# One LSTM with a picked cell: the input rows added by TensorE, and h split into three bf16 columns by GpSimd

## The reference

```python
g0 = x[:, 0] @ W_ih[0].T + b_ih[0] + b_hh[0]
h, c = _lstm_activate(g0, c0)
def step(carry, x_t):
    h, c = carry
    sel_in = jnp.concatenate([h, c, x_t], axis=-1)
    logits = sel_in @ W_sel.T + b_sel
    onehot = jax.nn.one_hot(jnp.argmax(logits, axis=-1), Sx, dtype=x_t.dtype)
    g_all = jnp.einsum('bi,sgi->bsg', x_t, W_ih) + jnp.einsum('bh,sgh->bsg', h, W_hh) + b_ih + b_hh
    g = jnp.einsum('bsg,bs->bg', g_all, onehot)
    h2, c2 = _lstm_activate(g, c)
```

## Time and profile before

| | |
|---|---|
| median of 3 runs | 6211.06 us |
| the profiled execution: its time, its span | 6218.48 us, 6216.4 us |
| granted TensorE clock, mean over the span | 0.944 |
| busy share PE, PEld, DVE, ACT, POOL | 87%, 52%, 49%, 17%, 10% |
| products of the cells (L1456) | 59,904, busy 1231.3 us |
| idle products (L1427) | 4,992, busy 1296.7 us |

### The profile page before, as it was taken

The page is one execution under the profiler, slowest core; times in us unless marked ns, Lnnn a source line. Parts: engine busy times, 40 slices in busy tenths (PEclk is TensorE's granted clock), DMA queues, the critical chain, the costliest instruction groups (busy, mean ns, idle before and its releaser), DMA issues. The chain is left out here.

```text
span 6216.4 us, 213415 instructions
## 1 busy us (share of the span) xinstructions
PE 5388.9 (87%) x84946; PEld 3259.5 (52%) x84948; DVE 3062.6 (49%) x13265; ACT 1070.7 (17%) x4645; POOL 612.3 (10%) x1014
## 2 busy tenths in 40 slices
PE   8998777848998929999999999999999999977778
PEld 6643443314666715555555555555555555544444
DVE  4401443213552165555555555555555555564543
ACT  0000000002331131111111111111111111122312
POOL 0000660001650000000000000000000000011100
PEclk9999998979999959999999999999999999988877
DMA  0000111467442230000000000000000000000010
GB/s 10 21 27 14 38 35 48 98 122 263 123 117 101 107 157 5 5 5 11 5 5 5 5 11 5 5 5 11 5 5 5 6 9 0 0 24 37 31 47 9
DMA packets 128787, 240.28 MB, mean 39 GB/s; under 512 B 47084, under 2 KB 64114, under 8 KB 127687
## 3 DMA queue, kind: packets, MB, share of 16 engines
q1 hardware_dynamic: 68584, 146.72, 6.7%
q0 software_dynamic: 60128, 92.58, 5.9%
HBM read 165.58 MB, written 73.29 MB: 38 GB/s over the span
## 5 line engine op out<-in xcount | busy, mean ns | idle before, releaser
L1456 PE MATMUL bank<-lstm_w,step_h_parts 128*32 128x128 f16 (+1 forms) x59904 | 1231.3, 237 | 174.3 <-issue 166.6
L1456 PEld LDWEIGHTS bank<-lstm_w,step_h_parts 128*32 128x32 f16 x59904 | 1116.0, 97 | 489.5 <-issue 480.0
L1427 PE MATMUL bank<-lstm_w 128*128 128x512 f16 x4992 | 1296.7, 382 | 3.8 <-issue 3.8
L1480 DVE TRANSPOSE_TENSOR_REDUCE step_summed<-bank 128x4 f32<-128x128 f32 x1872 | 669.7, 358 | 295.9 <-PE bank L1456 290.3
L1427 PEld LDWEIGHTS bank<-lstm_w 128*128 128x128 f16 x4992 | 386.2, 97 | 389.4 <-issue 5.7
L1406 ACT ACTIVATE step_act_out<-step_gates 128x4 f32<-128x4 f32 x625 | 128.5, 206 | 2091.2 <-DVE step_gates L1486 2087.7
L1486 DVE SCALAR_TENSOR_TENSOR step_gates<-step_summed,lstm_inv_scale,step_xgs 128x4 f32<-128x4 f32 x1872 | 415.0, 222 | 68.7
L1528 DVE COPY step_xgs<-step_xg 128x16 f32 x624 | 109.0, 175 | 688.5 <-issue 664.2
L1396 POOL COPY xnT<-step_state 128x4 f32 (+1 forms) x625 | 116.5, 186 | 3111.3 <-DVE step_state L1511 3111.3
L1109 PE MATMUL bank<-sum_parts,sum_hot 125*125 125x512 f16 x1600 | 347.3, 380 | 6.5 <-DVE sum_parts L1068 6.5
L1109 PEld LDWEIGHTS bank<-sum_parts,sum_hot 125*125 125x125 f16 x1600 | 219.1, 137 | 135.0 <-DVE sum_parts L1068 7.3
(11 more groups left out here) (368 smaller groups left out, 6563.8 us busy)
## 6 DMA issues: line engine op xcount, KB each, us to landing
rel_h<-rel_h_sb SPq DMA_DIRECT2D x39, 1024.0 KB, 4.3
lstm_xg<-xg_g POOLq DMA_DIRECT2D x4, 5000.0 KB, 19.5
step_xg<-lstm_xg SPq DMA_DIRECT2D x25, 800.0 KB, 4.4
xg_w<-in_c_w_ih SPq DMA_DIRECT2D x8, 2048.0 KB, 10.8
lstm_w<-in_c_w_hh SPq DMA_DIRECT2D x4, 4096.0 KB
rel_z<-rel_z_sb POOLq DMA_DIRECT2D x8, 1250.0 KB, 22.6
rel_zg<-rel_z POOLq DMA_DIRECT2D x8, 1248.0 KB
cheb_w<-in_L_gnn_weight SPq DMA_DIRECT2D x8, 1024.0 KB
```

The source lines that it names most:

```text
L1427: nc.tensor.matmul(idle[:], w[:, 0, 0, 0, 0, 0:128], w[:, 0, 0, 0, 0, :], start=True, stop=True)
L1456: last = nc.tensor.matmul(bank[32 * q:32 * q + 32, 0:32 * (end - first)], h_parts[:, c, :], w[:, s, c, q, a, 32 * first:32 * end], start=( ...
L1480: nc.vector.tensor_reduce(summed[:, first:end], bank[:, 0:32 * (end - first)].rearrange("p (b r) -> p b r", r=32), X_AXIS, ALU.add, apply_ ...
```

## The change

- `lstm_inputs`: the operands change places (x is stationary, 80 tiles of 125 steps by 512 gate columns, 4 products each). Each result is split into three bf16 parts by ScalarE and VectorE and stored by GpSimd's queue, 80 stores of 384 KB; the bias is split and stored alone. The weights come in 16 loads of 1 MB.
- `lstm_steps`: `xg` holds on its 128 partitions, for 15 steps, the three parts of every gate quarter and cell and, on other partitions, the same of the bias. One product per gate with a constant 0/1 matrix (`rows`) writes input and bias of all four cells into the gate's bank (`inject`); the cell's products add onto it with start=False. Gates are four parts of equal size in the order f, g, i, o.
- `h` is multiplied by `L.inv` when it is made, so the sums need no scale. The high column is VectorE's, and the middle and low ones are made by GpSimd; all are bf16. The weights stay float16 in two parts.
- L1486 (scale and add) and the copy of `xgs` are gone; VectorE's sum reads the picked cell's 128 columns by a register. The idle products go from 4 + 4 to 2 + 0, and four `inject` products are added, two before the pick and two behind the cell.
- `add_hidden` multiplies by `L.scale`.

```diff
-CHUNK = 25
-RING = 3 * CHUNK
+WARM_PICK = 2
+XG_CHUNK = 5
+XG_SLOTS = 3
@@ lstm_inputs, tensor
+            for i in range(TILES):
...
                 for c in range(KC):
-                    wt = w[:, n % 2, c, i % (GC // 2), :]
-                    nc.tensor.matmul(B.bank[2 * (i % 4)][:, 0:CUT], wt, xnT[:, c, 0:CUT], start=(c == 0),
-                                     stop=(c == KC - 1))
-                    last = nc.tensor.matmul(B.bank[2 * (i % 4) + 1][:, 0:N - CUT], wt, xnT[:, c, CUT:N],
+                    last = nc.tensor.matmul(B.bank[i % 6][0:R, :], xnT[:, c, m * R:(m + 1) * R], w[:, n % 2, c, :],
                                             start=(c == 0), stop=(c == KC - 1))
@@ lstm_steps, sync
+            def load(k, slot):
+                sp.dma_start(xg[0:XG_ROWS, bass.ds(slot * XG_CHUNK, XG_CHUNK), :],
+                             xg_rows[:, bass.ds(k * XG_CHUNK, XG_CHUNK), :]).then_inc(xg_loaded, 16)
+
+            sp.dma_start(rows_f[:], I["c_xg_rows"]).then_inc(rows_loaded, 16)
+            sp.wait_ge(cleared, 1)
+            sp.dma_start(xg[64:64 + XG_ROWS, :, :], bias_rows.to_broadcast((XG_ROWS, XG_RING, 512))
+                         ).then_inc(bias_loaded, 16)
@@ lstm_steps, gpsimd
             def keep(t, n):
-                pool.wait_ge(h_ready, n)
+                pool.wait_ge(h_hi_ready, n)
+                nc.gpsimd.tensor_tensor(h_rest[:], state[:, 4:8], h_parts[:, :, 0], ALU.subtract).then_inc(h_rest_ready, 1)
+                pool.wait_ge(h_rest_ready, 1)
+                pool.sem_inc(h_rest_ready, -1)
+                nc.gpsimd.tensor_copy(h_parts[:, :, 1], h_rest[:]).then_inc(h_mid_ready, 1)
+                pool.wait_ge(h_mid_ready, n)
+                nc.gpsimd.tensor_tensor(h_parts[:, :, 2], h_rest[:], h_parts[:, :, 1], ALU.subtract
+                                        ).then_inc(h_lo_ready, 1)
                 nc.gpsimd.tensor_copy(L.h[:, bass.ds(t * 4, 4)], state[:, 4:8]).then_inc(h_kept, 1)
@@ lstm_steps, tensor
+            def inject(part, at, stop):
+                p, bank, _, _ = part
+                return nc.tensor.matmul(bank[:], rows[:, p, :], xg[:, at, :], start=True, stop=stop)
...
                 last.then_inc(score_done, 1)
-                keep_clock_up(WARM_PICK - 1)
-                pe.wait_ge(init, 1)
+                inject_i_o(t)
+                keep_clock_up(WARM_PICK)
+                pe.wait_ge(picked, 1)
                 pe.wait_ge(h_lo_ready, t)
-                keep_clock_up(1)
-                pe.wait_ge(picked, 1)
                 s = pe.value_load(pick[0:1, 0:1])
...
-                keep_clock_up(WARM_GATES)
+                if ahead:
+                    inject_f_g(t + 1)
@@ lstm_steps, vector
-            def add_input(part, t):
-                first, end, _, _, summed_part, gates_part = part
-                dve.wait_ge(summed_part, t)
-                nc.vector.scalar_tensor_tensor(out=gates[:, first:end], in0=summed[:, first:end],
-                                               scalar=L.inv[:, 0:1], in1=xgs[:, first:end], op0=ALU.mult,
-                                               op1=ALU.add).then_inc(gates_part, 1)
...
-                nc.vector.scalar_tensor_tensor(out=state[:, 4:8], in0=act_out[:, 12:16], scalar=H_SCALE, in1=tc[:],
+                nc.vector.scalar_tensor_tensor(out=state[:, 4:8], in0=act_out[:, 12:16], scalar=L.inv[:, 0:1], in1=tc[:],
                                                op0=ALU.mult, op1=ALU.mult).then_inc(h_ready, 1)
                 dve.wait_ge(h_ready, n)
                 nc.vector.tensor_copy(h_parts[:, :, 0], state[:, 4:8]).then_inc(h_hi_ready, 1)
-                dve.wait_ge(h_hi_ready, n)
-                nc.vector.tensor_tensor(h_parts[:, :, 1], state[:, 4:8], h_parts[:, :, 0], ALU.subtract
-                                        ).then_inc(h_lo_ready, 1)
+
+            def parts_taken():
+                dve.sem_inc(done_f, -1)
+                dve.sem_inc(done_g, -1)
+                dve.sem_inc(done_i, -1)
+                dve.sem_inc(done_o, -1)
...
-                dve.wait_ge(xg_loaded, (t // CHUNK + 1) * 16)
-                nc.vector.tensor_copy(xgs[:], xg[:, bass.ds(s, 1), bass.ds((t % RING) * GC, GC)]
-                                      ).then_inc(xgs_ready, 1)
```

More of the change, by code:

```diff
@@ L1247, in lstm @@
         L.raw = sb("w", [128, BLOCKS + SHIFT, 512], F32)
+        L.scale = sb("scale", [128, 1], F32)
         L.inv = sb("inv_scale", [128, 1], F32)
@@ L1359, in lstm_steps @@
+    w = L.raw[:, 0:BLOCKS, :].bitcast(F16).rearrange("p (s c q) (a k) -> p s c q a k", s=CELLS, c=KC, a=2)
+    part_f = (0, B.bank[0], done_f, summed_f)
+    part_g = (1, B.bank[1], done_g, summed_g)
+    part_i = (2, B.bank[2], done_i, summed_i)
+    part_o = (3, B.bank[3], done_o, summed_o)
+    parts = (part_f, part_g, part_i, part_o)
+    score = B.bank[4][0:1, 0:8]
+    idle = B.bank[5]
+    halves = [(c, a) for c in range(KC) for a in range(2)]
     with ExitStack() as here:
-        xg = sb("xg", [128, CELLS, RING * GC], F32)
@@ L1423, in _, with add_half, cell @@
         def _(pe):
+            def inject(part, at, stop):
+                p, bank, _, _ = part
+                return nc.tensor.matmul(bank[:], rows[:, p, :], xg[:, at, :], start=True, stop=stop)
+            def add_half(part, s, c, a, stop):
+                p, bank, _, _ = part
+                for q in range(4):
+                    last = nc.tensor.matmul(bank[32 * q:32 * q + 32, 128 * s:128 * s + 128], h_parts[:, c, :],
+                                            w[:, s, c, q, a, 128 * p:128 * p + 128], start=False, stop=stop,
+                                            tile_position=(0, 32 * q))
+                return last
+            def cell(s):
+                for part in parts:
+                    for c, a in halves:
+                        last = add_half(part, s, c, a, stop=(c == KC - 1 and a == 1))
+                    last.then_inc(part[2], 1)
             def keep_clock_up(products):
@@ L1427, in keep_clock_up, with inject_f_g, inject_i_o, step @@
                     nc.tensor.matmul(idle[:], w[:, 0, 0, 0, 0, 0:128], w[:, 0, 0, 0, 0, :], start=True, stop=True)
-            pe.wait_ge(init, 1)
-            with pe.Fori(1, STEPS) as t:
-                pe.wait_ge(init, 1)
-                pe.wait_ge(input_score_ready, t)
+            def inject_f_g(t):
+                at = bass.ds(t % XG_RING, 1)
+                for part in (part_f, part_g):
+                    pe.wait_ge(part[3], t)
+                    inject(part, at, stop=False)
+            def inject_i_o(t):
+                at = bass.ds(t % XG_RING, 1)
+                for part in (part_i, part_o):
+                    pe.wait_ge(part[3], t)
+                    last = inject(part, at, stop=False)
+                last.then_inc(injected, 1)
+            def step(t, ahead=True):
+                pe.wait_ge(input_score_ready, 1)
+                pe.sem_inc(input_score_ready, -1)
                 nc.tensor.matmul(score[:, 0:CELLS], B.ones[0:1, 0:1], input_score[:], start=True, stop=False)
```

301 lines of the change are left out of this document (164 added, 137 removed).

## The result

The kernel with the change takes **6305.4 us** (median of 4 runs, 6300.33 to 6311.18), the kernel before beside it 6213.06 (4 runs, 6207.29 to 6216.94): ratio 1.0148, interval 1.0136 to 1.016. It is slower by 92 us. The forecast was 6141, and the range ended at 6290. The profiled execution took 6311.18 us, its span is 6309.4.

What follows compares the result with a forecast made beforehand. The prediction took the LSTM step's ring of dependent instructions as the bound: step 2.05 + 2.91 = 4.96 against 5.08 us, times 624 = -75, +5 around the loop, 6148 profiled, 6141 us median; range 5990 to 6290.

Steps and rivals of the forecast that it cites:

- The ring and what bounds it: One LSTM step, from H (start of the instruction making h) to next H: 5.08 us, forecast 4.96, times 624.
- From S to the next h: From S, the start of the cell's products, through sums, ig, c and tanh to h: 2.91 us instead of 3.37.
- The low column at H+1.25: GpSimd's three new instructions, 0.19 us each plus links, make h's last column ready 1.25 us after h's instruction starts.
- The cell starts 0.80 after the later one: TensorE's register load and branches: cell starts 0.80 us after the later of pick and low column, S = H+2.05.
- The pick at H+1.0: VectorE's lookup of the largest score: known at H+1.0 instead of H+0.91, the loop's branch now ahead of it.
- Around the loop +5: Stages outside the steps: first weight load -5, input products +6, end -2, loop's start +6 us; sum +5.
- Idle products, clock, SP: TensorE's replaced idle products and SP's loads cost nothing; clock stays 1.00. Rival of falling clock: 6249 us, chance 0.07.
- GpSimd's chain is longer than I take: Rival, between high column and TensorE's reading of the pick: 0.17 a link, H+1.45, 6266 us; decides from H+1.37; chance 0.16.
- Instructions twice VectorE's: Rival, same place: GpSimd's three instructions 0.35 us each, low column at H+1.73, step 5.44, 6441 us; chance 0.04.
- its sums might stay bound by VectorE's queue: Rival that the change does not do what it says: sums start at H+2.62 at best, 6203 us; chance 0.08.
- The forecast's own range of 6070 to 6215: Range of the main case, chance 0.50: GpSimd links between 0.07 and 0.13, instructions between 0.16 and 0.22.
- the lower bound's S: Cell's start with GpSimd instructions of 98 ns and the pick deciding: H+1.78, step 4.69, -243 us.

Runs made afterwards that it cites:

- the best version: Changed kernel with two f16 columns by VectorE, search at loop's end, semaphores taken after each sum, GpSimd-copy wait behind h, last step in loop: 5922.83 us, ratio 0.953.

## Why the prediction was wrong

Against the path the forecast used, step by step:

- **The ring and what bounds it: right.** From S to the next h 2.91 was forecast, 2.92 measured, with the sums at S+0.68 (0.69 forecast) and 0.45 apart in the timeline. The size hides two misses that cancel, so that it came out so near is in part luck. In the timeline c starts at S+2.41 instead of 2.48, since ig took 0.12 instead of 0.16 and began a little sooner; and from tanh to h it was 0.31 instead of 0.23. The change also puts the wait for GpSimd's copy of h ahead of h, where it stood ahead of c; the diff, which shows only parts, does not have it, and I did not price it. By its place it makes an instruction of the wait for tanh. The run that took it away from there gave back 40 us. Ahead of c it cost the same before: the earlier trace rows has 0.27 from ig to c, and the forecast put 0.20 there without saying why.
- **The low column at H+1.25: too early by 0.13.** This is the larger part of what failed, 0.13 x 624 = 81 us. Three terms of this sum were mis-sized. H to the end of the high column was taken as 0.37 from the earlier trace rows, but h's instruction now reads its scale from memory (`L.inv` for a constant) and takes 0.22 instead of 0.16 (0.16 again with a constant, in the best version): 0.06. The GpSimd instructions took 0.20, 0.20 and 0.22 instead of 0.19, the copy of the earlier trace rows: 0.05 together. The links took 0.08, 0.17 and 0.08 instead of 0.09, 0.13 and 0.09: 0.02 together.
- **"The cell starts 0.80 after the later one": 0.89.** This is the smaller part in size, 0.09 x 624 = 56 us, but a term for which the forecast allowed no error. With 0.80 the late column would have made the step 5.10, hardly over the 5.07 of before. 0.80 was read behind the pick, whose wait the load carries. Two waits stand ahead of the load, and the late one had become an instruction of its own, 0.10 ahead of the load. The run that turned the order round gave 64 us back.
- **The pick at H+1.0: 1.15.** The search begins with MAX8, at H+0.49 before, and not with the instruction at 8.42 that the forecast named. The loop's branch and its register instructions hold the search back by 0.23 (0.49 to 0.73), more than the 0.1 taken. It is hidden, as the run with the earlier search shows.
- **The sum.** S is 0.22 late (0.13 and 0.09), S to H 0.01 longer, and the step before was 5.07 and not 5.08. So the step is 0.124 longer than before instead of 0.12 shorter: 624 x 0.244 is 152 us. With 7 us for the last step and about 4 more around the loop than the 5 forecast, 6141 becomes 6304; measured is 6305.
- **Around the loop +5.** The input rows went better than forecast: their first product starts at 1900.2 instead of 1907.7, and their last at 2176.8 instead of 2178.6, so 276.6 us against 270.9, which is the +6 forecast. The stage ends 3.9 us sooner. The loop's start was dearer: 10.6 us more until the first h where 6 were taken. ScalarE's ACT_TABLE_LOAD of 1.28 us, which ran during the wait for the first load before (2299.8), now stands behind the first sum (2309.6). TensorE's way out of the loop, 7 us, was not thought of.
- **Idle products, clock, SP: right.** 1.00 in all stretches of the loop; without idle products it is 0.88 to 0.93.

Of the rivals, "GpSimd's chain is longer than I take" is the one that came, with its place and its deciding point of H+1.37 (measured 1.38), but in part for other reasons: the long link it feared was one of three, and its price of 6266, for a column at H+1.45, left out the 0.09 behind the chain. Instructions twice VectorE's did not come: a subtraction of 4 columns takes GpSimd 0.20 and 0.22 us, where VectorE took 0.17 and 0.18 for the same two in the run with its own three columns. The ratio of the Trainium skill, page "GPSIMD Engine Reference", section "Performance versus the Vector engine", does not hold at this size; that of these rows is about 1.2. The change also did what it says; that its sums might stay bound by VectorE's queue is refuted: in the median step they start 0.05 behind the end of each quarter of the products and 0.45 apart.

The range was too narrow at its upper end: it let links and instructions vary, but took the 0.80 behind them and the 0.37 ahead of them as fixed. The forecast's own range of 6070 to 6215 is narrower than its terms as well: links of 0.13 and instructions of 0.22 throughout give H+1.42, a step of 5.13 and 6247 us, and links of 0.07 with instructions of 0.16 give H+1.06 and 6023. And with the pick deciding at H+1.0, the lower bound's S is 1.80 and not 1.78.

## What to carry to other kernels

Where the time is a ring of short instructions, price every instruction on the ring, the semaphore instructions included: look which of two waits the waiting instruction carries itself (here the one written first, on TensorE and on VectorE), let it be the one that is met last, and put waits that have long been met where the engine is idle anyway. A chain of dependent small instructions on a second engine costs its number of links (0.28 to 0.37 us each here), not its work; one that ends before something else does costs little or nothing (6219 against 6212 us), three on the path cost their links. When a part of a change is right and another wrong, separate them: against the kernel before, the best version gains 290 us; three bf16 columns by GpSimd took 268 of it, and the places of two waits, the last step and the late search another 115.

## What was not expected of the hardware

- Of two waits ahead of one instruction the one written second was an instruction of its own. Where it was the one met last, it cost TensorE 0.10 us ahead of its load (load at H+1.53 against 1.42) and VectorE 0.07 ahead of h (S to H 2.92 against 2.85).
- An operand read from memory instead of a constant: VectorE's instruction for h 0.22 us against 0.16, ScalarE's on a gate 0.297 against 0.205.
- The clock gave way in steps in which TensorE stood still 1.20 us ahead of the cell (granted 0.96 to 0.97) and, without idle products, 1.33 us (0.88 to 0.93), while 0.92 us of standing still with two idle products left it at 1.00.
- A part of TensorE's code that runs once behind a loop cost 7 us in the trace: 5.1 of waiting and 1.9 because the clock fell to 0.50 behind the wait.
